# Zeros only behind each expert's last row, six early attention jobs, and three scatters in flight from the first

## The reference, cut to what matters

```python
xn = _layernorm(x, axis=-1)
x = x + attn(xn, ...) + ffn(xn, ...)

# ffn
topk_idx, topk_weight = _gate(hs, gate_weight, e_score_correction_bias)      # 6 of 16 experts a token
comb = jnp.zeros((T, E)).at[jnp.arange(T)[:, None], topk_idx].add(topk_weight)
for e in range(E):
    g = hs @ gate_proj[e].T                                                  # 256 -> 176
    u = hs @ up_proj[e].T
    out = out + comb[:, e:e + 1] * ((jax.nn.silu(g) * u) @ down_proj[e].T)   # 176 -> 256
sg, su = hs @ shared_gate_w.T, hs @ shared_up_w.T                            # 256 -> 352
shared_out = (jax.nn.silu(sg) * su) @ shared_down_w.T

# attention: qkv = tok @ qkv_w on 16-channel tokens; windows of 8; softmax(q k^T) v plus a 3-tap
# convolution of v; a 16x16 projection, a layer norm over 16 channels, added to the token
```

## Time and profile before

| | |
|---|---|
| device time, median of 3 executions | 509.59 us (505.76 to 511.91) |
| the profiled execution | 503.04 us |
| its span, first to last instruction | 501.3 us |
| PE busy | 410.9 us (82%) |
| DVE busy | 360.7 us (72%) |
| ACT busy | 224.9 us (45%) |
| POOL busy | 233.7 us (47%) |
| mean granted TensorE clock | 0.913 of 2.4 GHz |
| moved by DMA | 91.55 MB, mean 183 GB/s |

### The profile page before, as it was taken

One profiled execution on the slowest core, in us unless ns is written; L12 is line 12 of the kernel. 1 busy time (PEld: TensorE's weight loads), 2 busy tenths in 40 slices (PEclk: granted clock), 3 DMA queues, 4 the chain that ended last, 5 costly groups with the idle time before them and its releaser, 6 DMA issues.

```text
span 501.3 us, 7250 instructions
## 1 busy us (share of the span) xinstructions
PE 410.9 (82%) x1989; PEld 313.3 (63%) x1989; DVE 360.7 (72%) x587; ACT 224.9 (45%) x616; POOL 233.7 (47%) x221
## 2 busy tenths in 40 slices
PE   7897999981988969999998999898963399999500
PEld 7776998971656647677776777675642177766300
DVE  3779827860897758999999999999830034568971
ACT  3752453260454324655667655753531244464300
POOL 2702236656687756850000000078777345467572
PEclk9897999995999969999999999999995599999955
DMA  7999977654455635668533333366665376454553
GB/s 182 351 350 388 412 257 266 209 170 154 146 165 175 210 122 177 197 191 239 148 111 90 97 109 110 93 175 180 184 184 146 86 202 180 128 156 146 167 161 90
DMA packets 65957, 91.55 MB, mean 183 GB/s; under 512 B 8448, under 2 KB 57344, under 8 KB 65664
## 3 DMA queue, kind: packets, MB, share of 16 engines
q1 hardware_dynamic: 54144, 63.02, 41.0%
q0 software_dynamic: 9216, 25.96, 16.6%
q10 hardware_dynamic: 2560, 2.10, 1.5%
HBM read 43.48 MB, written 47.57 MB: 182 GB/s over the span
## 4 chain that ended last, share of the span: by engine, by line
PE 36%; DVE 23%; issue 13%; DMA 12%; another core or an unknown queue 6%; ACT 3%; POOL 3%; SPq 1%; DVEq 1%; POOLq 0%
PE gate L980 13%; PE ps_y L1003 11%; DMA xs_dram<-xrow,slot_i 10%; DVE prod L1083 4%; PE ps_y L996 4%; PE up L970 3%; DVE sc L1083 3%; DVE qkv L1083 3%; DVE inter_s L1505 3%; DVE yacc L1587 2%; POOL xs_dram L585 2%; PE misc L1030 2%; SPq L427 1%; DVE yacc L1571 1%
## 5 line engine op out<-in xcount | busy, mean ns | idle before, releaser
L980 PE MATMUL gate<-wrec,xgT 128*128 x444 | 155.2, 473 | 1.1 <-DVE inter_s L1505 0.8
L585 POOL DMA_INDIRECT xs_dram<-xrow,slot_i x96 | 109.0, 1136 | 66.7 <-DMA xs_dram<-xrow,slot_i 30.3
L1003 PE MATMUL ps_y<-wrec,interT 88*128 x444 | 117.8, 389 | 0.0
L605 POOL DMA_INDIRECT gat<-y_dram,slot_i x50 | 55.9, 1118 | 132.5 <-DMA y_dram<-y_s 105.0
L1505 DVE SCALAR_TENSOR_TENSOR inter_s<-gate,xg,gate_s 128x176 f32<-128x176 f32 x111 | 43.7, 394 | 88.5 <-ACT gate_s L722 69.9
L980 PEld LDWEIGHTS gate<-wrec,xgT 128*128 128x128 f32 x444 | 77.9, 195 | 27.5 <-issue 4.6
L1003 PEld LDWEIGHTS ps_y<-wrec,interT 88*128 88x128 f32 x444 | 77.6, 195 | 7.0 <-issue 0.3
L722 ACT ACTIVATE gate_s<-gate 128x176 f32<-128x176 f32 x111 | 35.3, 318 | 89.5 <-PE ps_y L996 47.0
L996 PE MATMUL ps_y<-ident,inter_s 128*88 128x128 f32 x222 | 43.5, 279 | 34.4 <-issue 15.9
L742 ACT ACTIVATE y_s<-ps_y 128x256 f32<-128x256 f32 x107 | 41.0, 383 | 66.2 <-PE up L970 37.8
L996 PEld LDWEIGHTS ps_y<-ident,inter_s 128*88 128x88 f32 x222 | 25.7, 124 | 71.1 <-issue 41.7
(11 more groups left out here) (210 smaller groups left out, 626.7 us busy)
## 6 DMA issues: line engine op xcount, KB each, us to landing
xg<-xs_dram SPq DMA_DIRECT2D x111, 136.0 KB
y_dram<-y_s SPq DMA_DIRECT2D x111, 128.0 KB
xs_dram<-zrow SPq DMA_DIRECT2D x1, 9384.0 KB, 34.0
wrec<-wexp SPq DMA_DIRECT2D x14, 608.0 KB
xs_dram<-zrow SPq DMA_DIRECT2D x14, 408.0 KB
xn_dram<-xrow SPq DMA_DIRECT2D x8, 256.0 KB, 3.2
qkv<-xn_dram SPq DMA_DIRECT2D x8, 256.0 KB
xs_dram<-xrow,slot_i POOLq DMA_INDIRECT x96
```

Of the source, the lines that this page charges most:

```text
L585: nc.gpsimd.indirect_dma_start(xs_dram[0:DONE[max(d for d in DONE if d <= c)] * P, :], bass.IndirectOffsetOnAxis(slot_i[:, o:o + 1], 0), x ...
L605: nc.gpsimd.indirect_dma_start(places[place_of(n)][:, there:there + H], None, y_dram[0:DONE[max(d for d in DONE if d <= first)] * P, :], b ...
L980: last = nc.tensor.matmul(guA[t % 2][:, 0:2 * I], xgT[:, t % 2, k * P:(k + 1) * P], wrec[:, bass.ds(record + k * 2 * I, 2 * I)], start=(k ...
L1003: last = nc.tensor.matmul(ps_y[:, t % 2 * 2 * H:t % 2 * 2 * H + H], interT[:, t % 2, k * P:(k + 1) * P], wrec[0:HALF, bass.ds(record + KT ...
```

## The change

1. **Zeros only where rows may be missing.** SP first writes 16 tiles of zeros over tiles 96 to 111 (one more tile than NT is allocated). Everything else is left unwritten but for 16 DMAs of 128 rows of zeros, one for each expert, from the row behind the expert's last one. Where that is, DVE computes in six new small instructions in `routing` (into `pad_row`, semaphore `pads_ok`); SP loads the 16 numbers into registers, four at a time, and issues the 16 DMAs (`pad_zeros`). The first scatter waits for all of them. The 14 DMAs of 3 tiles and their waits are gone. `ROUTE_PLAN` has one step more behind unit 1.
2. **Six early jobs.** `FIRST_JOBS` is 6: jobs 0 to 5 run ahead of the prefix matmuls, in three banks in turn, so that jobs 3 to 5 wait for the copies of jobs 0 to 2. Rounds 0 to 4 have two jobs each, none between up and down.
3. **Three in flight.** `FLIGHT_AHEAD` is 3.

```diff
-FLIGHT_AHEAD, FLIGHT = 2, 3
+FLIGHT_AHEAD, FLIGHT = 3, 3
-FIRST_JOBS = 3
+FIRST_JOBS = 6
-ROUTE_PLAN = {-1: 23, 0: 1, 1: 17, 2: 14, 3: 12, 4: 12}
+ROUTE_PLAN = {-1: 23, 0: 1, 1: 18, 2: 14, 3: 12, 4: 12}
+FULL = T * TOP // P
@@ late_jobs
-    n = FIRST_JOBS + (0, 2, 4, 7, 10)[s]
-    return ((n,), (), (n + 1,)) if s < 2 else ((n,), (n + 1,), (n + 2,))
+    n = FIRST_JOBS + 2 * s
+    return (n,), (), (n + 1,)
@@ SP
-            zero_tiles(sp, 0, DONE[0], first_zeros)
+            zero_tiles(sp, FULL, NT + 1, tail_zeros)
             for e in range(TAIL):
                 sp.dma_start(wrec[:, e * REC:(e + 1) * REC], wexp[:, e * REC:(e + 1) * REC]).then_inc(w_in, 16)
-            for n, t in enumerate(range(DONE[0], NT, ZT)):
-                sp.wait_ge(m_ok, ZEROS_AT + n * (UNITS - ZEROS_AT) // ((NT - DONE[0]) // ZT))
-                zero_tiles(sp, t, t + ZT, more_zeros)
+            sp.wait_ge(pads_ok, 1)
+            sp.wait_ge(tail_zeros, 16)
+            regs = [sp.alloc_register(f"pad_at{i}") for i in range(4)]
+            for e in range(0, NE, 4):
+                nc.sync.load(regs, pad_row[0:1, e:e + 4])
+                for reg in regs:
+                    row0 = nc.sync.snap(reg, min_val=0, max_val=NT * P)
+                    sp.dma_start(xs_dram[bass.ds(row0, P), :], zrow[:, :]).then_inc(pad_zeros, 16)
@@ POOL
-            pool.wait_ge(first_zeros, 16)
+            pool.wait_ge(pad_zeros, 16 * NE)
-                if n == MARKS[1] * TOP:
-                    pool.wait_ge(more_zeros, 16 * ((NT - DONE[0]) // ZT))
@@ PE, qkv_job
-                    before = -1
+                    before = n - 3
                 elif n < EARLY_JOBS:
-                    before = n - 1 if n > FIRST_JOBS else 0
+                    before = n - 1 if n > FIRST_JOBS else FIRST_JOBS - 3
@@ DVE, routing, behind the tile starts
+                inner, end, base = (begins_left[0:1, a:b] for a, b in ((0, (PARTS - 1) * NE), ((PARTS - 1) * NE, PARTS * NE),
+                                                                      (PARTS * NE, (PARTS + 1) * NE)))
+                do(nc.vector.tensor_tensor(inner.rearrange("p (n e) -> p n e", e=NE),
+                                           upto[0:1, NE:PARTS * NE].rearrange("p (n e) -> p n e", e=NE),
+                                           upto[0:1, PARTS * NE:].unsqueeze(1).to_broadcast([1, PARTS - 1, NE]), ALU.is_lt))
+                do(nc.vector.tensor_scalar(base, upto[0:1, PARTS * NE:], 1.0, float(P), ALU.max, ALU.mult))
+                tt(inner, inner, work[0:1, later], ALU.mult)
+                settle()
+                do(nc.vector.tensor_reduce(end, inner.rearrange("p (n e) -> p e n", e=NE), AX.X, ALU.add))
+                settle()
+                do(nc.vector.scalar_tensor_tensor(end, end, -1.0 - P, shift[0:1, NE:2 * NE], ALU.add, ALU.add))
+                settle()
+                nc.vector.tensor_tensor(pad_row[:, :], end, base, ALU.add).then_inc(pads_ok, 1)
+                yield
```

More of the change, by code:

```diff
@@ L234, in build @@
         e_row = at("e_row", [1, RT], I32)
+        pad_row = at("pad_row", [1, NE], I32)
         blk_at = cursor[0]
@@ L306, in build @@
         cst_in, xn_out = sem("cst_in"), sem("xn_out")
-        first_zeros, more_zeros = sem("first_zeros"), sem("more_zeros")
+        tail_zeros, pads_ok, pad_zeros = sem("tail_zeros"), sem("pads_ok"), sem("pad_zeros")
         xn_in, out_sp, out_act, w_in, tail_in = sem("xn_in"), sem("out_sp"), sem("out_act"), sem("w_in"), sem("tail_in")
@@ L340, in build @@
         seg = sc[:, HD * P - TOK * NE:]
+        begins_left = sc[:, 5 * (PARTS + 1) * NE:HD * P - TOK * NE]
         xw = xrow[:, :].rearrange("p (c w) -> p c w", w=XW)
@@ L416, in zeros_left @@
         def zeros_left(engine):
-            engine.wait_ge(first_zeros, 16)
-            engine.wait_ge(more_zeros, 16 * ((NT - DONE[0]) // ZT))
+            engine.wait_ge(tail_zeros, 16)
+            engine.wait_ge(pad_zeros, 16 * NE)
         def load_x(engine, n, b_of):
```

6 lines of the change are left out of this document (2 added, 4 removed).

## The result

The changed kernel takes **525.13 us** (median of 4 runs, 521.63 to 529.37) beside 507.67 us of the kernel before on the same chip (504.91 to 511.91): a ratio of **1.034, 95% interval 1.021 to 1.047**. The forecast was 495 us. The sign was wrong.

A forecast was written before the change was run, and what follows sets the result against it. Scatters, ending 12 us after PE's own work, were taken to hold up the tile loop; 13.2 + 1.5 = 14.7 us off 503.04 gives 488.3 profiled, plus 6.55 gives 494.9, say 495 us timed; range 483 to 504.

The forecast's parts named there:

- The pads: Before the scatters: numbers ready at 47.6, register loads 1.6 us, 16 copies 9.6 us, first scatter at 61.0.
- The rival in which the pads hold everything up: Before the first scatter: pads at 2.7 us each put xg at 139.8, total 527 us; chance 0.05.
- The scatters: Ahead of the tile loop: 1.40 us each, the 30th starting at 101.6 and xg there at 106.2.
- PE's own chain up to 109.4: Shared units before the tile loop: PE's last attention job ends at 109.4 in place of 110.74.
- the prediction's own last sign of being wrong: The forecast is wrong if, among other signs, new waits stand in the shared units; no size given.
- The main step, 13.2 us: Start of the tile loop: at 109.4 in place of 122.61, 13.2 us earlier.
- a spacing of up to 1.51 us: Scatters before the tile loop: the 3.2 us of slack behind xg hides a spacing up to this.
- The first rival: Tile loop: if dense scatters cause ACT's stalls of 3.58 and 4.96 us, 8.5 us more go, 486.4; chance 0.22.
- The third rival: Scatters don't land faster with three in flight, or stalls move into the shared units: 507.7 us; chance 0.09.
- The full clock from the start: Tile loop's first 10 us: full granted clock, since PE comes from full work without the pause.
- the 1.5 us of this term: Tile loop's first steps: 1.5 us gained without the idleness that lowered the clock, bounds 0.6 and 2.6.
- The six jobs, 1.3 us: Shared units: three jobs move ahead of the prefix, and rounds 2 to 4 gain 1.3 us in all.

The follow-up runs named there:

- e1: The kernel before with three scatters in flight from the first, nothing else changed: 498.21 us, ratio 0.984.
- e2: The changed kernel with two scatters in flight for the first 40, as before: 499.43 us, ratio 0.988 to the kernel before.
- e4: The changed kernel with two short waited memsets on POOL behind each of the first 42 scatters: 515.29 us, ratio 1.019 to the kernel before.
- e3: The kernel before with six early jobs, nothing else changed: 505.25 us, ratio 0.998.
- e5: The changed kernel with one short waited memset on POOL behind each of the first 42 scatters: 495.54 us, ratio 0.980 to the kernel before.
- e6: The kernel before with one short waited memset on POOL behind each gather of the first 18 fetches: 510.07 us, ratio 1.011.
- e10: e5 with two waited memsets behind each gather of the first 18 fetches, on the fast chip: 482.29 us, ratio 1.039 to the kernel before.
- e11: The changed kernel with rests of 12 waited memsets behind scatters 12, 24 and 36, on the fast chip: 452.48 us in one run, 0.975 to the kernel before.
- bursts_again: e11's kernel run again, on a fourth chip, of the slower kind: 499.36 us, ratio 0.984 to the kernel before.

## Why the prediction was wrong, point by point

- **The pads, right.** The six small DVE instructions end at 47.71, forecast 47.6. Here are the last of them (DVE) and SP's issues:

```profile
47.55 0.16 DVE L1313 TENSOR_TENSOR pad_row<-sc 1x16 int32<-1x16 f32 x1
```

```profile
48.47 9.88 SPq L466 DMA_DIRECT2D xs_dram<-zrow  x16
```

  The 16 copies and their loads take 9.9 us, forecast 1.6 + 9.6 with the first load ahead of them; the first scatter starts at 60.14, forecast 61.0. The rival in which the pads hold everything up gave 527 us, near the result, and had nothing to do with it.
- **The scatters, right and better.** Forecast 1.40 us each and the 30th at 101.6; 1.29 and 97.43. Less traffic and three in flight do let POOL run unbraked. e1 and e2 show that either alone doesn't (1.73, 1.57).
- **PE's own chain up to 109.4, wrong, and this is the step that failed.** The forecast took PE's work in the shared units as independent of POOL: the terms behind "PE's last job ends at 109.4" are jobs, DVE's low part and the clock. PE's last job came at 152.8, after 38.3 us of idleness that the sum had at nothing; the prediction's own last sign of being wrong, new waits in the shared units, came true. The working of PE's own work was sound: with scatters at 2.1 us the job ends at 109.1 (e4, e3), in e5 at 108.1, in the other paced runs at 110 to 118. POOL's pauses, in front of most scatters, had been counted as loss to be removed, and they were what let PE's announcements through in time.
- **The main step, 13.2 us.** With the stall removed and little else changed (e5) the loop starts at 112.0 in place of 122.6, 10.6 us, and the time falls by 2.0 and 1.7% where 2.9% was forecast. The size was near; the condition, a pace that PE's announcements keep up with (1.5 us or more in the table), was missing. The prediction had "a spacing of up to 1.51 us" as what the *slack* allows; it had no lower bound.
- **The first rival, "ACT's stalls go as well".** It found the right place: unexplained waits in a stretch of dense scatters, and asked whether the density causes them. Its conclusion was the wrong way round: if so, denser scatters at a place where PE has no slack make more of them. The third rival said in half a sentence that the stalls could move into the shared units, put it at 507.7 in all, without a working of its own, and gave it a share of 0.09. The trace had 8.5 us of such stalls beside 33 scatters at 1.44 us; at 1.27 us PE lost 38.3. The loop itself did get shorter, by 11.1 us (PE busy 6.6 us less, at a granted clock of 0.96 in place of 0.94, idle 4.4 less), since the first 42 scatters were long out when it began.
- **The full clock from the start came true, in a place where it proves little.** The granted clock was 0.50 (1.2 GHz) from 82.5 us on, after PE's first pauses (0.34 to 1.03 us, from 78.11 on), to 126.8; the loop then began without a pause, at 1.00 from 152 to 162 where before had 0.75 from 122 to 132. No run gives the 1.5 us of this term by themselves.
- **The six jobs, 1.3 us**: 1.6 in PE's last job (e3), nothing in the time, as long as the scatters come last.

## What to carry to other kernels

A wait in front of a DMA issue can be what the other engines live on. Before taking the last brake off a queue of indirect DMAs, look in the trace for the stretch in which they already run unbraked, see whose semaphore updates are late there, and price these waits at the new place, where they may have no slack. Then set the pace on purpose: three in flight *and* a short wait behind each scatter gave 2% where the same kernel without it lost 3.4%. And judge such a change on several chips.

## What the hardware showed that I had not expected

- While POOL issues 128-row indirect DMAs every 1.27 us for 50 us, PE's semaphore updates come up to 42 us late, and PE's own matmuls come apart, at 111 GB/s of traffic. DVE's, ACT's and POOL's updates never do. At 1.36 (the gathers of e6) PE's are late too, at a mean of 1.5 to 1.7 it idles for 1 to 8 us, at 2.1 us nothing of that shows. Twelve in a row with 3.7 us to the next cost 1.9 us.
- It differs between chips. On four of them the kernel before takes 502 to 507 us (and 508 in the first comparison, whose chip isn't on record), on a fifth 464. There e10 and e11 have no late release, though 12 scatters ran there at 1.27 us in a row and the gathers at their full pace. The changed kernel itself wasn't run on it; whether it stalls there, or gains the 3% that were forecast, stays open.
- Recording itself is a rival that no run excludes. Every run on record has its span and clock from a recording. And records are lost where updates are late: the trace of bursts_again holds 6,471 semaphore updates and that of e11, the same kernel on the chip without late ones, 10,269. In the changed kernel's first trace the updates of 103 of 577 DVE instructions are missing, none of them before 60 us or from 260 to 340, where POOL issues little or nothing; on the fifth chip 2 are. Whether PE's updates are late without recording stays open.
- The cause underneath isn't settled. The runs tell rate from number in flight; they don't tell whether it is the descriptors that POOL writes, the completions, or something in the path of the semaphores. Writing fewer bytes a row at the same rate, which would have told bytes from issues, wasn't tried. The Trainium skill has rules that fit either: "DMA: Bandwidth & Descriptors" (Why a DMA increments its semaphore by 16 and not by 1) says that for DMAs of this kind all 16 engines post an increment each, which at 1.27 us would be an increment every 0.08 us, an estimate from that page's 16 and the interval measured (e11's trace agrees with the 16: 254 to 256 landing records for the 16 scatters of each semaphore); and "VectorE: DVE Perf Modes" (the TRN2 errata) warns that dense semaphore increments of one engine can deadlock another and asks to space them. No run here shows a deadlock, nor that increments are the cause; that spacing helps, e5 and bursts_again show, and e4 for the stall alone.
